# The second layer's scores for the maxima, moved behind the value products and the side product of their slot

## What is computed

```python
xn = layernorm(x)                                   # layer 0
x = x + L0_attn(xn) + L0_ffn(xn)
xn = layernorm(x)                                   # layer 1
...
logits = jnp.einsum('bhqd,bhkd->bhqk', q, k) / SCALE
logits = logits - alpha[:, None, None] * dist[None]
attn = jax.nn.softmax(logits, axis=-1)
out = jnp.einsum('bhqk,bhkd->bhqd', attn, v)
...
top_w, top_idx = jax.lax.top_k(scores, TOP_K)       # two of 32 experts
y = jnp.einsum('etd,te->td', y_e, combine)
x = x + L1_attn(xn) + L1_ffn(xn)
```

## Time and profile before

| | |
|---|---|
| median of 3 runs | 1120.41 us (1119.45 to 1124.75) |
| span of the profiled execution | 1121.8 us, within the runs' range |
| first maxima of layer 1, last maxima of layer 1 | about 481 and 1065 us |
| PE busy / DVE busy / ACT busy, whole span | 894.3 / 823.4 / 664.2 us |
| mean granted TensorE clock | 0.937 of full |

### The profile page before, as it was taken

One profiled execution on the slowest core, in us unless ns is written; L12 is line 12 of the kernel. 1 busy time (PEld: TensorE's weight loads), 2 busy tenths in 40 slices (PEclk: granted clock), 3 DMA queues, 4 the chain that ended last, 5 costly groups with the idle time before them and its releaser, 6 DMA issues.

```text
span 1121.8 us, 29817 instructions
## 1 busy us (share of the span) xinstructions
PE 894.3 (80%) x12223; PEld 436.5 (39%) x12223; DVE 823.4 (73%) x1377; ACT 664.2 (59%) x1022; POOL 349.2 (31%) x415
## 2 busy tenths in 40 slices
PE   2687766998888897777876877778899899798966
PEld 1365543344444443333321323234444344344422
DVE  8979987778888888887889676762764674675624
ACT  3234322666666666634685676755667667666785
POOL 3433322221321321303031666603334244142230
PEclk9799996899999999988997999987999899999998
DMA  7900055334424424324141242542435544443044
GB/s 185 223 20 10 20 123 124 87 75 114 107 59 106 107 60 106 91 53 108 35 106 37 75 118 61 149 109 76 134 93 124 137 111 111 123 122 88 27 129 122
DMA packets 116012, 108.42 MB, mean 97 GB/s; under 512 B 14706, under 2 KB 108836, under 8 KB 115492
## 3 DMA queue, kind: packets, MB, share of 16 engines
q1 hardware_dynamic: 108772, 94.95, 33.4%
q0 software_dynamic: 7104, 11.57, 3.9%
HBM read 64.73 MB, written 48.35 MB: 101 GB/s over the span
## 4 chain that ended last, share of the span: by engine, by line
PE 44%; DVE 25%; ACT 11%; issue 8%; SPq 8%; DMA 2%; POOL 2%; ACTq 0%; DVEq 0%
DVE a_maxes L1521 11%; PE a_psO L1296 11%; ACT a_Pt L1371 5%; PE a_psS L1257 4%; PE a_psS L1277 4%; PE a_psM L1241 3%; SPq L1048 2%; PE a_psM L1316 2%; PE a_psM L1235 2%; PE a_psM L1168 2%; ACT a_Pt L1367 2%; SPq L1030 1%; PE f_ps_g L785 1%; PE f_ps_d L807 1%; SPq L1049 1%
## 5 line engine op out<-in xcount | busy, mean ns | idle before, releaser
L1521 DVE TENSOR_REDUCE a_maxes<-a_psS 128x2 f32<-128x1024 f32 (+3 forms) x432 | 506.4, 1182 | 167.5 <-PE a_psS L1141 164.9
L1371 ACT ACTIVATE a_Pt<-a_psS,alpha 128x512 f32<-128x512 f32 x512 | 315.2, 695 | 113.1 <-PE a_psS L1141 112.4
L1296 PE MATMUL a_psO<-a_Pt,V 128*32 128x512 f32 (+3 forms) x2048 | 241.0, 549 | 12.9 <-ACT a_Pt L1371 7.6
L1257 PE MATMUL a_psS<-K,Q 60*64 60x512 bf16 (+3 forms) x2048 | 178.9, 363 | 75.3 <-ACT a_Pt L1371 40.2
L1367 ACT ACTIVATE a_Pt<-a_psS 128x1024 f32<-128x1024 f32 (+1 forms) x176 | 163.9, 943 | 71.7 <-PE a_psS L1141 69.9
L1277 PE MATMUL a_psS<-Q,K 63*64 63x512 bf16 (+3 forms) x2048 | 178.1, 366 | 25.3 <-DVE a_maxes L1521 20.0
L1277 PEld LDWEIGHTS a_psS<-Q,K 63*64 63x64 bf16 x2048 | 58.9, 107 | 158.7 <-issue 80.0
L1257 PEld LDWEIGHTS a_psS<-K,Q 60*64 60x64 bf16 x2048 | 61.1, 111 | 148.5 <-ACT a_Pt L1371 58.5
L345 POOL TENSOR_TENSOR qkf<-qkf,parts 128x512 f32<-128x512 f32 x30 | 34.7, 1158 | 237.4 <-ACT parts L1342 237.4
L1656 POOL DMA_INDIRECT y<-spare,r_sent_id x64 | 61.5, 960 | 148.2 <-PE a_psS L1141 137.7
L1141 PE MATMUL a_psS<-dist,eye 64*64 64x64 bf16 x2048 | 105.4, 196 | 0.0
(11 more groups left out here) (242 smaller groups left out, 1269.8 us busy)
## 6 DMA issues: line engine op xcount, KB each, us to landing
stack<-parts SPq DMA_DIRECT2D x192, 128.0 KB
expert_w<-in_expert_w SPq DMA_DIRECT2D x96, 128.5 KB
Q<-stack SPq DMA_DIRECT2D x64, 192.0 KB
K<-stack SPq DMA_DIRECT2D x64, 192.0 KB
xs<-in_c_no_token SPq DMA_DIRECT2D x24, 258.0 KB, 6.1
slots_flat<-xs SPq DMA_DIRECT2D x24, 258.0 KB, 4.5
xnT<-xnT_dram SPq DMA_DIRECT2D x16, 256.0 KB, 3.1
slots_flat<-y SPq DMA_DIRECT2D x16, 256.0 KB, 4.6
```

Of the source, the lines that this page charges most:

```text
L1257: pe.matmul(banks[HEAD_ROWS * hf:HEAD_ROWS * (hf + 1), b, x * w:(x + 1) * w], Q[rows, k % 4, q, at:at + HEAD_ROWS], K[rows, k % 4, q, 0:w] ...
L1296: m = pe.matmul(psO[32 * j:32 * (j + 1), q0:T], V[:, (src - 2) // 2 % 2, kt, r, j, :], Pt[:, (nB.at(src) + unit) % RING, h % 2, x // 2 * w ...
L1371: m = act.activation(Pt[:, u % RING, b, :], scores[:, b, :], ACT.Exp, bias=0.0, scale=n.alpha[:, h:h + 1])
L1521: dve.tensor_reduce(maxes[:, k % 2, i, :, heads[0] // 2:heads[0] // 2 + pairs], src, AX, ALU.max, negate=True).then_inc(a_free, 1)
```

## The change

In steps with 16 slots that start a half (16 to 31) the item A of a slot no longer stands right behind B but behind the PV and the side products of the slot. A and B still take turns in the same order, so each waits for the same bank as before. Steps of layer 0 are as they were.

```diff
-        if s in units_a:
+        if s in units_a and not wide:
             out.append(("A", s))
         while groups and value_is_due(k, done_b, groups[0]):
             out.append(("PV", groups.pop(0)))
         out += here
+        if s in units_a and wide:
+            out.append(("A", s))
```

## The result

| | before | changed |
|---|---|---|
| median in the same comparison | 1119.93 us (1118.75 to 1124.75, 4 runs) | 1133.39 us (1129.27 to 1137.86, 4 runs) |
| ratio to before | 1 | 1.0122 [1.0079, 1.0165] |
| span of the profiled execution | 1121.8 us | 1130.4 us (its own time 1132.19) |
| PE / DVE / ACT busy | 894.3 / 823.4 / 664.2 us | 894.6 / 821.0 / 670.5 us |

The changed kernel is slower by 13.5 us by the medians. The forecast was 1126.6, slower by 6.2: the direction held, the range (up to 1134) held by 0.6 us, and the size was about half. No engine got more instructions, so the time went into waits.

The account below looks back on a forecast made before the run. Latency of the loop B, exponential, A, PV, B sets the pair, no engine's work. Terms 6.5 + 4.5 + 1.2 - 1.5 - 1.4 - 3.15 = +6.15 us gave 1126.6 us, range 1113 to 1134.

Parts of the forecast that it names:

- The plain pair: Slots that hold nothing else, steps 18 to 31: PV to PV 3.14 against 3.19 us, about 30 pairs, -1.5 us.
- Rival 1: PV behind B starts after 0.27, not 0.38, in about 110 intervals: -12 us, 1114.5 in all; chance 0.12.
- OT and EX: Slots where DVE takes out OT's division or the experts' tokens, steps 17 to 31: +0.3 each, +4.5 us.
- V's boundary: Value projection V in the last slot of steps 24, 26, 28 and 30: +0.3 each, +1.2 us.
- The key projection: PNK's stretch in step 22: PV to PV 4.27 against 5.00, -0.7; with step 20 -1.4 us.
- What the transfers absorb: Delays shorten PE's waits for loads in step 24 and odd expert steps 27 and 29: -3.15 us.
- Rival 2: No change: expert loads set more of steps 24 to 30, 3.5 us more absorbed, 1123; chance 0.13.
- rival 4: PE falls to 1.2 GHz in the plain steps: 24 us for steps 21 and 23, 1151; chance 0.02.
- I take nothing beyond the terms above: Steps 16 to 19: no extra loss or gain counted, DVE having the same rows in order and nearly full.
- the prediction's own sign of being wrong: Prediction is wrong if, among other signs, steps 16 to 19 together move by more than 4 us.
- The upper end that the text itself worked out: Steps 16 to 19: a loss if each maximum waits for side work as in OT's slot, 64 x 0.3 = 19 us.
- The start of the step: PV7 to PV0, with MS ahead of the first maxima: +0.55 in eight odd, +0.3 in seven even steps, +6.5 us.

Follow-up runs that it names:

- only_16_19: The new order of A in steps 16 to 19 alone, steps 20 to 31 in the old one; 1126.06 us, 1.0068 of the kernel before.
- from_20: The changed kernel with steps 16 to 19 in the old order, the new order in steps 20 to 31 alone; 1126.84 us, 1.0050 of the kernel before.
- oc_first: The changed kernel with OC, ACT's copy of the finished outputs, ahead of B and its exponentials in slot 2; 1120.73 us, 1.0024 of the kernel before.
- pv_only: The changed kernel with only the value products ahead of A, the side products behind it as before the change; 1127.61 us, 1.0101 of the kernel before.
- before_oc_first: The kernel before, in its own order of A, with OC ahead of B in slot 2 alone; 1124.49 us, 1.0061 of the kernel before.
- oc_v_ot_20: oc_first with steps 16 to 19 in the old order, V of slot 15 and OT of odd plain steps behind A again; 1118.72 us, 0.9995 of before.

## Why the prediction was half the size

Right, by its own steps:

- **The plain pair.** Worked out 3.14, measured 3.14 in all but one of them, with B's wait for the maxima (0.80) in the place of A's for ACT. Rival 1, a PV that starts sooner behind B, is refuted: PV comes 0.37 behind B (712.84 to 713.21), and 0.38 was taken.
- **OT and EX.** Worked out 4.09 against 3.77, measured 4.06, and 4.01 for EX. V's boundary: taken +0.3, measured +0.36 (4.63 against 4.27). The key projection: worked out 4.27, measured 4.20.
- **What the transfers absorb.** Taken 3.15, measured 2.9 (4.6 to 3.1 and 6.8 to 5.4), and 5.0 in the second profiled execution (3.0 and 3.4). Rival 2, which needed 6.65 and a time of 1123, is refuted.
- **The clock in plain steps**, rival 4: 1.00 in step 21, as before. What the Trainium skill tells of another kernel (TensorE: Matmul & The Clock Gate, "A second HAM failure mode: psum-queue depth-cycling") does not show in this step in either order, with an idle 0.87 before A or 0.84 before B in each pair.

Wrong:

- **"I take nothing beyond the terms above"** for steps 16 to 19 is the step that failed. Its general terms give these four steps some 2.3 us (two odd starts, one even, OT's price three times); only_16_19 lost 0.0068 of 1119, 7.6 us [3.9, 11.3]. By the middle of that interval it is the prediction's own sign of being wrong, a move of more than 4 us, and the range held only because its ends had been drawn apart for these steps. The argument was that DVE has the same rows in the same order and is nearly full. The rows are the same and the order is not: the side work moved ahead of the maxima of its slot, and B waits for those. The upper end that the text itself worked out, each maximum waiting for its side work as in OT's slot, was the right mechanism, at some slots. Rows of before could have shown it: all 7 of B's waits for the maxima lay in these four steps, so DVE was already what PE waited for there, and the slot sums and the second norm's rows still stood behind the maxima of their slots.
- **The start of the step**, +0.55 and +0.3, was mis-sized. Odd steps measured +0.65 to +0.69 (19, 21, 23) and +0.80 to +0.81 (25 to 31), the even ones +0.36 and +0.39 (18, 22) and +0.59 (26, 28, 30). Over these twelve starts that is 7.7 where the terms had 5.4. In step 23, 0.13 comes from one number. MS was put 1.14 behind the start of the maxima ahead of it, from a row in which it stood behind maxima that it does not need. It now stands behind the ones it does need and comes 1.27 behind their start (711.55 to 712.82): the whole reduction must be done first. In the odd expert steps V's copies are ahead of it as well; what they add is not shown apart.
- **The number of plain pairs** was mis-sized, too. Some 30 were taken, for -1.5 us; 19 intervals of 3.18 stand in steps 18 to 31, and together they gained 0.4 us.

For steps 20 to 31 the forecast's share, 6.15 - 2.3 = 3.85, lies inside what from_20 measured, 5.6 us [1.2, 10.0]. So of the 7 us that were missing, some 5 belong to steps 16 to 19 by the middle of that interval, and some 2 to the starts.

How the 7.6 us of steps 16 to 19 split among their slots is only partly shown: the two places above carry 2.2, the general terms as measured 1.6 (the starts of 18 and 19, 1.0, and OT twice 0.3), and two more intervals of step 18 and one of step 19 that grew 0.17, 0.31 and 0.31 carry 0.8. The whole of steps 18 and 19 can be read from their value products: from PV0 of step 18 to PV0 of step 20 it is 70.4 and 71.7 us in the changed kernel's two profiled executions and 71.8 in only_16_19, where it is 65.9 to 66.9 in the five kernels with A in its old place there. These two steps alone lose some 4 to 6 us. The rest would lie in steps 16 and 17, where the profiled executions of one kernel differ by as much (58.3 and 62.2 us from PV0 of step 16 to PV0 of step 18); it stays open.

## What to carry to other kernels

When an item of one engine's queue moves, list what stands behind it in the queues of the engines that read it, and which of those reads has a deadline: here the maxima changed sides with MS, OT's division, V's copies, the second norm's rows and the router's sums, and each of them became a wait of PE. A wait that goes away in a ring of banks can go to the next member of the ring: here the pair of slots won 0.05 us where 0.87 us of waiting vanished. And a latency taken from a row holds only for the same dependence: behind work that it merely follows in the queue MS started sooner (1.14 us after the start of the maxima) than behind work whose result it reads (1.27).

## What was not expected of the hardware

The same kernel differs from one execution to the next by where PE's clock falls to its lower level. The two profiled executions of the changed kernel spanned 1130.4 and 1116.4 us. Their windows from 520 to 550 us (columns as in the earlier trace rows), first that of the execution with 1130.4:

```profile
520.00:550.00 30.00, 22.82 (x380) 9.38 (x380) 26.47 (x47) 14.15 (x21) 0.00 (x0) 0.77 0.39 85
```

and that of the one with 1116.4:

```profile
520.00:550.00 30.00, 20.95 (x388) 8.77 (x389) 26.15 (x42) 17.44 (x27) 0.00 (x0) 1.00 0.33 65
```

At a mean granted clock of 0.77 the stretch holds time at 1.2 GHz, at 1.00 it is all at 2.4; PV0 of step 18, just behind it, takes 1.94 us and not 1.06, and the interval from it to the next PV is 5.39 against 4.07. Over 207 runs of the comparisons, a fit with one constant for each kernel and one slope on the mean granted clock gives -7.5 us for each 0.01 of clock, and leaves 1.9 us of scatter; the kernel before ran from 1110.72 us at 0.955 upwards. At equal clock the changed kernel lies 10.5 us above the one before, only_16_19 6.3, from_20 5.5 and oc_first 3.1. So up to 3 us of the 13.5 may be a draw of clocks. The two halves of the change stay as they were found, and oc_first still takes back most (7.4 of 10.5), but not every finding stays: at equal clock pv_only lies 12.9 us above the kernel before and so above the changed kernel, before_oc_first only 3.2, and oc_v_ot_20 2.2 under it [1.0, 3.4]. This does not make oc_v_ot_20 faster: the clock may itself depend on the order of the work, and no run here separates the two.
